# The maxima of the first two query blocks, computed inside the projection stage instead of at the head of the attention stage

## The reference, cut to what matters

```python
q = (x @ Wq).reshape(b, n, 4, 4, 32); k = (x @ Wk).reshape(b, n, 4, 32); v = ...
scores = einsum('bqgsd,bkgd->bgsqk', q, k) / sqrt(32)
scores = where(key > query, -inf, scores)
attn = softmax(scores, axis=-1)
ctx = einsum('bgsqk,bkgd->bqgsd', attn, v).reshape(b, n, 512)
x = layernorm(x + ctx @ Wo + bo)
mu_n = mu / max(sqrt(sum(mu * mu, axis=0)), 1e-12)      # one length per slot, 16 x 128 slots
```

## Time and profile before

| | us |
|---|---|
| median of 3 runs | 2527.34 (2526.09 to 2530.71) |
| the profiled execution, its own time | 2529.19 |
| its span in the profile | 2527.5 |
| projections, until the barrier | 0 to 167.8 |
| attention, until the last product of context and its way out | 167.8 to about 1170 |

### The profile page before, as it was taken

How to read it: one execution, slowest core, us unless ns; L and a number is a source line. 1 busy time by engine, 2 the same in 40 slices (tenths; PEclk the granted TensorE clock), 3 DMA queues, 4 the chain that set the end, 5 groups by cost and what they waited for, 6 DMA issues and landing times. The chain is left out here.

```text
span 2527.5 us, 39129 instructions
## 1 busy us (share of the span) xinstructions
PE 2426.7 (96%) x13026; PEld 1731.5 (69%) x13026; DVE 1738.8 (69%) x3805; ACT 1427.4 (56%) x2764; POOL 1758.0 (70%) x1723
## 2 busy tenths in 40 slices
PE   8989999999999999996978999999999997999998
PEld 6865555555555555543767888877888886788886
DVE  3338888888888888833876656566656564867776
ACT  3214566666666666663865655566656563454553
POOL 4403979898989999897957676675575765555553
PEclk9988999999999999998989999999999998999999
DMA  7861121212222121103964445476444457664553
GB/s 250 271 199 34 40 62 40 62 46 61 57 53 54 50 52 47 49 9 123 361 199 146 160 133 167 138 222 186 142 151 151 144 161 248 190 224 132 148 152 101
DMA packets 232666, 329.58 MB, mean 130 GB/s; under 512 B 56560, under 2 KB 102672, under 8 KB 228240
## 3 DMA queue, kind: packets, MB, share of 16 engines
q1 hardware_dynamic: 195856, 283.47, 36.8%
q0 software_dynamic: 35968, 43.06, 5.8%
q10 hardware_dynamic: 640, 0.55, 0.1%
HBM read 180.63 MB, written 112.22 MB: 116 GB/s over the span
## 5 line engine op out<-in xcount | busy, mean ns | idle before, releaser
L1033 ACT ACTIVATE p_probs<-p_ps_s 128x512 f32<-128x512 f32 (+3 forms) x1280 | 588.9, 540 | 325.8 <-PE p_ps_s L955 320.9
L1624 POOL DMA_DIRECT2D p_eT<-p_ex x1024 | 538.5, 535 | 274.7 <-DVE p_ex L1890 222.1
L884 POOL TENSOR_TENSOR p_added<-p_added,p_probs 128x2048 f32<-128x2048 f32 x136 | 623.9, 4587 | 10.8
L1064 DVE TENSOR_REDUCE p_parts<-p_ps_m 128x1 f32<-128x512 f32 x768 | 468.8, 678 | 45.4 <-PE p_ps_m L942 44.2
L955 PE MATMUL p_ps_s<-q,k_e 98*128 98x512 f32 (+3 forms) x1280 | 472.9, 389 | 3.5 <-ACT p_probs L1033 3.3
L942 PE MATMUL p_ps_m<-k_m,q 96*128 96x512 f32 (+3 forms) x1280 | 455.0, 386 | 7.7 <-PEq L2165 3.9
L955 PEld LDWEIGHTS p_ps_s<-q,k_e 98*128 98x128 f32 x1280 | 241.9, 191 | 180.3 <-issue 82.9
L942 PEld LDWEIGHTS p_ps_m<-k_m,q 96*128 96x128 f32 x1280 | 245.8, 194 | 79.2 <-DVE p_parts L1064 23.6
L973 PE MATMUL p_ps_c<-p_probs,v_e 128*32 128x512 f32 (+3 forms) x2560 | 276.7, 539 | 1.8 <-POOL p_probs L864 1.8
L2024 POOL TENSOR_TENSOR p_acc<-p_acc,logit 128x512 f32<-128x512 f32 x112 | 164.2, 1466 | 151.1 <-ACT logit L2077 147.7
L1068 DVE CUSTOM_DVE_ANT_0 p_masked<-p_ps_m,p_mask 128x384 f32<-128x384 f32 (+3 forms) x512 | 220.5, 485 | 53.7 <-PE p_ps_m L942 47.1
(11 more groups left out here) (193 smaller groups left out, 4772.5 us busy)
## 6 DMA issues: line engine op xcount, KB each, us to landing
logits_t<-logit SPq DMA_DIRECT2D x32, 1024.0 KB, 5.0
p_eT<-p_ex POOLq DMA_DIRECT2D x1024, 32.0 KB, 2.0
logit<-logits_t SPq DMA_DIRECT2D x128, 256.0 KB, 3.4
q<-q_t SPq DMA_DIRECT2D x96, 256.0 KB, 4.7
c_first<-L_ffn_W_dram SPq DMA_DIRECT2D x64, 256.0 KB, 5.6
p_x<-L_attn_x_dram SPq DMA_DIRECT2D x32, 256.0 KB, 5.2
q_t<-p_f_hi SPq DMA_DIRECT2D x32, 256.0 KB, 5.5
q_t<-p_f_lo SPq DMA_DIRECT2D x32, 256.0 KB, 5.6
```

The lines of the kernel that those rows point to most:

```text
L884: pool.tensor_tensor(a[:, :, :], first[:, :, :], probs[s % RING][:, :, :], ALU.add).then_inc(s_add, 1)
L1033: act.activation(probs[s % RING][:, h, q0:BLK], ps_s[:, u % ST_BANKS, q0:BLK], ACT.Exp).then_inc(s_exp, 1)
L1064: dve.tensor_reduce(to, bank, AX.X, ALU.max).then_inc(s_taken, 1)
L1624: pool.dma_start(eT[r][p * QD:(p + 1) * QD, i, :, :], ex[i * QD:(i + 1) * QD, 2 * r:2 * r + 2, bass.ts(p, P)]).then_inc(s_eT[r], 16)
```

## The change

- The constant AHEAD = 2 names the query blocks whose maxima move. Their 48 units (U0 = 48) leave the planner's list and stand in the projections instead, spread over 36 places: behind each chunk c of the groups m = 2 to 5 of block 6 and m = 0 to 4 of block 7. They use the banks `ps_t`, free after the transposes of the last block. The first four wait for VectorE's `xT_lo`, and each later one for the fourth unit before it.
- VectorE does the 48 reductions and both blocks' `maximum_rows` in the projections, each group's reductions ahead of that group's `f_lo`. Mask and scratch lie in an input tile that is no longer used, and GpSimd writes the mask there after its sums.
- The rows of block 0 go out on SP's queue inside the last block's stores (4 DMAs), those of block 1 on ScalarE's at the end of the stage (4 DMAs).
- The attention list starts with unit 48 and with the scores of step 0. `slot_lengths` is now in the plan, after unit 95, in a `ps_m` bank; VectorE copies it out, and GpSimd takes it to the power -0.5 after it has normalised block 1. The load of Wo and the store of the lengths stand behind the context store of block 2 on SP's queue. ScalarE no longer takes a root.
- The semaphore of the first loads is split by block, so a unit or a score waits for its own block only; the wait for all stores is put in front of TensorE's first context product.

```diff
--- before.py
+++ after.py
@@ -94,6 +94,11 @@
         m_in = [al.sbuf(f"p1_mu{j}", [P, DC, EQ * S]) for j in range(2)]
+        mask, masked = x_in[0][:, 0, :], [x_in[0][:, 1 + r, :] for r in range(3)]
+        parts = [al.sbuf(f"p1_parts{n}", [P, 16, QB]) for n in range(AHEAD)]
+        pairs = al.sbuf("p1_pairs", [P, 16, 2])
+        split = al.sbuf("p1_split", [P, 32], F32R)
+        s_row, rows = early
         ps_t = al.psum("p1_ps_t", DC)
...
@@ -117,8 +125,24 @@
+        places = [(NBLK - 2, m, c) for m in range(2, VT + 1) for c in range(DC)] + [(NBLK - 1, m, c) for m in range(VT) for c in range(DC)]
+
+        def units_behind(blk, m, c):
+
+            if (blk, m, c) not in places:
+                return []
+            at, count = places.index((blk, m, c)), M_END[AHEAD - 1]
+            return list(range(at * count // len(places), (at + 1) * count // len(places)))
+
         block = ctx.enter_context(nc.Block())
         x_b = x.rearrange("b n c -> (b n) c")
+
+        def send_rows(eng, n):
+
+            eng.wait_ge(s_max, n + 1)
+            for a in range(4):
+                to = first[0][QROWS:MROWS, n, :, :].rearrange("o h (t a j) -> o h t a j", t=4, a=4)[:, :, :, a, :]
+                eng.dma_start(to.bitcast(F32), rows[n][a * 32:(a + 1) * 32, :]).then_inc(s_row[n], 16)
...
@@ -132,6 +156,8 @@
                 for m in range(NF):
+                    if blk == NBLK - 1 and m == 2:
+                        send_rows(sp, 0)
                     for half, src, ready, done in ((0, f_hi, s_fhi, s_ohi), (1, f_lo, s_flo, s_olo)):
...
@@ -194,6 +220,11 @@
                     load_mu(k + 2)
+            pool.wait_ge(s_xt, (NBLK - 3) * DC)
+            pool.memset(mask, 0.0).then_inc(s_mask0, 1)
+            pool.wait_ge(s_mask0, 1)
+            pool.affine_select(out=mask[:, BLK - P:], in_=mask[:, BLK - P:], compare_op=ALU.is_ge, fill=MASKED,
+                               base=0, pattern=[[-1, P]], channel_multiplier=1).then_inc(s_mask, 1)
             pool.wait_ge(s_mst, 16 * 8)
...
@@ -238,7 +269,24 @@
                                             xT_hi[j][:, c, :], xT_lo[j][:, c, :], c == 0, c == DC - 1)
+                        for u in units_behind(blk, m, c) if c < DC - 1 else []:
+                            unit(u)
                     last.then_inc(s_f, 1)
+                    for u in units_behind(blk, m, DC - 1):
+                        unit(u)
+
+            def unit(u):
+
+                n, c, t, h = MAXU[u]
+                w = unit_width(u)
+                if t == 0 and h == 0 and c == n:
+                    pe.wait_ge(s_first[c], 160)
+                if u < DC:
+                    pe.wait_ge(s_xlo, (NBLK - 1) * DC + u + 1)
+                else:
+                    pe.wait_ge(s_taken, u - DC + 1)
+                pe.matmul(ps_t[:, u % DC, 0:w], first[0][0:QROWS, n, h, bass.ts(t, P)], first[1][:, c * BLK:c * BLK + w],
+                          start=True, stop=True).then_inc(s_unit, 1)
...
@@ -291,6 +339,8 @@
                 values(blk)
+            for n in range(1, AHEAD):
+                send_rows(act, n)
...
@@ -308,6 +358,9 @@
                 for m in ms:
+                    for c in range(DC):
+                        for u in units_behind(blk, m, c):
+                            maximum(u)
                     dve.wait_ge(s_fhi, blk * NF + (m + 1))
...
@@ -320,6 +373,35 @@
                 dve.tensor_copy(v_out[blk % 2][:, :, :], ps_f[:, (FB * blk + V) % 4, :]).then_inc(s_v, 1)
+
+            def maximum(u):
+                n, c, t, h = MAXU[u]
+                w = unit_width(u)
+                to, bank = parts[n][:, h * 4 + t, c:c + 1], ps_t[:, u % DC, 0:w]
+                dve.wait_ge(s_unit, u + 1)
+                if c < n:
+                    dve.tensor_reduce(to, bank, AX.X, ALU.max).then_inc(s_taken, 1)
+                else:
+                    if u == 0:
+                        dve.wait_ge(s_mask, 1)
+                    if u >= 3:
+                        dve.wait_ge(s_taken, u - 2)
+                    dve.tensor_tensor_reduce(masked[u % 3][:, 0:w], bank, mask[:, BLK - w:], 1.0, -3.0e38, ALU.add, ALU.max,
+                                             to).then_inc(s_taken, 1)
+                if u + 1 == M_END[n]:
+                    maximum_rows(n)
+
+            def maximum_rows(n):
...
+                dve.transpose(rows[n][:, :], split[:, :].bitcast(F32)).then_inc(s_max, 1)
...
@@ -331,6 +413,9 @@
                 features_lo(blk, range(2, NF))
+                for c in range(DC):
+                    for u in units_behind(blk, VT, c):
+                        maximum(u)
             values(NBLK - 1)
...
@@ -355,6 +440,9 @@
 MOVING = 4
+AHEAD = 2
+U0 = M_END[AHEAD - 1]
+FIRST_MASKED = min(u for u in range(U0, NU) if MAXU[u][1] == BLOCKS[MAXU[u][0]][1])
...
@@ -433,6 +521,7 @@
         self.work, self.moves = [], []
+        self.rows.update((n, 0.0) for n in range(AHEAD))
         self.groups, self.stall = 0, {"m": 0, "s": 0, "c": 0, "r": 0}
...
@@ -505,6 +594,14 @@
             self.moves.append((self.maxed[u], "maxima keys", (it + 1, c)))
+
+    def lengths(self):
+        self.matmul(self.bank_free(), P)
+        self.pe += 1000
+        self.work.append(("lengths", 0, None))
+        self.dve = max(self.dve, self.pe + self.LAND + self.HOP) + 150
+        self.freed.append(self.dve)
+        self.work.append(("flip lengths", 0, None))
...
@@ -675,6 +772,8 @@
             u += 1
+            if u == M_END[AHEAD]:
+                k.lengths()
         elif add_up:
...
@@ -828,13 +932,16 @@
                 sp.wait_ge(s_ov[j], 16 * NBLK // 2)
-            sp.wait_ge(s_nsum, 1)
-            sp.dma_start(w_raw[:, :, :], Wo.rearrange("(g p) c -> p g c", p=P)).then_inc(s_wo, 16)
             for _, what, a in transfers():
...
                     store(a)
+                    if a == AHEAD:
+                        sp.wait_ge(s_nsum, 1)
+                        sp.dma_start(w_raw[:, :, :], Wo.rearrange("(g p) c -> p g c", p=P)).then_inc(s_wo, 16)
+                        sp.wait_ge(s_ninv, 1)
+                        sp.dma_start(d["inv"], n_inv[:, :]).then_inc(s_nout, 16)
                     if a == NBK - QB:
...
@@ -914,6 +1022,10 @@
                     normalise(a)
+                    if a == AHEAD - 1:
+                        pool.wait_ge(s_pow, 1)
+                        pool.wait_ge(s_flip, flips_to("lengths", 0))
+                        pool.tensor_tensor(n_inv[:, :], n_max[:, :], power[:, :], ALU.pow).then_inc(s_ninv, 1)
                     if a in WEIGHT_BLOCKS:
...
@@ -939,6 +1051,8 @@
                         pe.wait_ge(s_km[c], 48 * it)
+                if t == 0 and h == 0 and it == 0 and c == 0:
+                    pe.wait_ge(s_first[qb], 160)
                 pe.matmul(ps_m[:, bank("maximum", u), 0:w], q[0:QROWS, qb, h, bass.ts(t, P)], k_m[:, c * BLK:c * BLK + w],
...
@@ -948,7 +1062,9 @@
                     pe.wait_ge(s_row[qb], 64 * it + 64)
-                    if it > 0:
+                    if it == 0:
+                        pe.wait_ge(s_first[qb], 160)
+                    else:
                         pe.wait_ge(s_ke[qb], 48 * it)
...
@@ -994,23 +1110,27 @@
             def slot_lengths():
+                at = bank("lengths", 0)
                 pe.wait_ge(s_ones, 1)
                 pe.wait_ge(s_nin, 16)
                 for e in range(E):
-                    mm = pe.matmul(ps_c[:, 0, e:e + 1], mu_sq[:, bass.ts(e, S)], ones[:, 0:1], start=True, stop=True)
+                    mm = pe.matmul(ps_m[:, at, e:e + 1], mu_sq[:, bass.ts(e, S)], ones[:, 0:1], start=True, stop=True)
                 mm.then_inc(s_nsum, 1)
-            pe.wait_ge(s_first, 16 * 10 * QB)
             for what, a, h in order():
                 if what == "maximum":
-                    if a == 12:
-                        slot_lengths()
                     unit(a)
+                elif what == "lengths":
+                    slot_lengths()
                 elif what == "scores":
...
                     if a == 0:
-                        pe.wait_ge(s_nlen, 1)
+                        for m in range(GROUPS + 1):
+                            pe.wait_ge(s_ohi[m], 16 * NBLK)
+                            pe.wait_ge(s_olo[m], 16 * NBLK)
+                        for j in range(2):
+                            pe.wait_ge(s_ov[j], 16 * NBLK // 2)
                     context(a)
...
@@ -1038,10 +1158,6 @@
-            act.wait_ge(s_nsum, 1)
-            act.activation(n_len[:, :], ps_c[:, 0, 0:E], ACT.Sqrt).then_inc(s_nlen, 1)
-            act.wait_ge(s_ninv, 2)
-            act.dma_start(d["inv"], n_inv[:, :]).then_inc(s_nout, 16)
             for what, a, h in order():
...
@@ -1107,15 +1225,12 @@
-            dve.wait_ge(s_mask, 1)
             for what, a, h in order():
                 if what == "maximum":
                     maximum(a)
-                    if a == 23:
-                        dve.wait_ge(s_nlen, 1)
```

(6 more changed lines are left out.)

71 lines of the change are left out of this document (45 added, 26 removed).

## The result

The changed kernel takes 2515.5 us (median of 8 runs, 2510.9 to 2523.5) against 2529.2 us before (8 runs, 2526.1 to 2531.3): ratio 0.9949, 95% interval [0.9935, 0.9962], or 13.7 us less. I had forecast 2508, a gain of 19.9 by its sum, from a kernel before whose median then stood at 2527.3 (3 runs); so 1.9 of the 7.5 us between 2508 and 2515.5 is the kernel before; the gain itself fell short by 6.2 (the sum came to 2507.4). On a second chip the same pair gave 0.9945 [0.9932, 0.9957]. The profiled execution of the changed kernel took 2523.5 us, the longest of its eight.

What follows compares the result with a forecast made beforehand. TensorE, busy 96% of the span, was taken as the bound. 2529.2 less 29.6 at the attention head plus 9.7 in the projections gave 2509.3, 2507.4 on the medians' scale, stated as 2508 us; range 2498 to 2521.

Steps and rivals of the forecast that it cites:

- the 17 us that I gave it: Attention stage: no exp for about 17 us from some 32 us into the stage.
- The projections: Stage before attention: the 48 moved units make it 9.7 us longer, bounds 8 and 14.
- the tie: Projections: VectorE 3.9 us against TensorE 4.0 per full-width group of chunks; 1.1 us added for it.
- My chain through SP: Projections' end: SP's queue ends the stage; 6.0 us of units plus 2.6 for block 0's four row DMAs, 8.6.
- ScalarE's four are beside this: Projections' end: four DMAs on ScalarE's queue lie beside SP's chain and add nothing to it.
- Stretch 1: Head of the attention stage, to the rows of block 2: 48 units, 43 scores, 7 context products; 30.7 us, bounds 27 and 34.
- Stretch 2: Attention stage, run of 28 units after the lengths with one score, set by VectorE: 18.4 us, bounds 17 and 21.
- the one for the lengths: Lengths ahead of the 28-unit run: 3.5 us on TensorE at full clock, filled banks covering 1.8, 1.5 added.
- Stretch 3: Attention stage, from the 28-unit run to the sending of block 3's rows: 31.4 us, bounds 27 and 36.
- The lead is kept: Attention stage after block 3's rows: both lists run on with TensorE full, lead unchanged, 3 us either way.
- the mark: Issue of block 3's rows, where both lists read alike: 80.5 us into the attention stage against 110.1, 29.6 less.
- a tenth of its time free later: Attention stage: GpSimd's mask and power of the lengths cost nothing, as it has a tenth of its time free.
- The middle rival, half the gain: Projections 14 more and stretch 3 at 36 us: 2516 us; with stretch 1 at 34, 2520; chance 0.14.

Runs made afterwards that it cites:

- x4: Changed kernel with block 0's row DMAs in a gap of ScalarE's, half of block 1's on SP, and the lengths' power at block 9's normalisation: 0.9946, 2517.9 us.
- x3: Changed kernel with AHEAD = 1, so only block 0's 16 units stand in the projections: 0.9968, 2523.0 us.
- x0: The changed kernel unaltered, run again with a second profile: 0.9945, 2518.8 us on a chip where the kernel before takes 2532.7.
- x11: Changed kernel with one matmul in place of the sixteen of the slot lengths, fifteen sums left out (results wrong): 0.9928.
- x2: Changed kernel with the slot lengths moved behind block 7's rows, and GpSimd's power and the two DMAs hanging on them at block 6: 0.9929.
- x7: Changed kernel with GpSimd's adds of blocks 0 to 4, from each block's third tile on, cut to a quarter of their columns (sums wrong): 0.9928, 2513.5 us.
- x10: Changed kernel with GpSimd's power of the lengths moved right behind VectorE's copy of the lengths out of their bank: 0.9923.
- x8: The kernel before, unaltered, with a second profile; rows of block 3 at 281.2 us instead of 277.9.
- x9: Changed kernel with x4's row DMAs, block 0's late sums issued as soon as ready, and the power right behind VectorE's copy of the lengths: 0.9901, 2506.6 us.

## Why the prediction was right in sign and 7.5 us off

**The mechanism** was as forecast: exps start with the stage (177.85), they pause, the projections pay TensorE's time for the units at full clock. The pause is longer than the 17 us that I gave it: but for one exp at 210.04 there is none from 204.6 to 233.95 us.

**The projections**: 9.7 forecast, 8.8 measured. The 8.3 us of the units on TensorE is the term that counts: its last transposes start at 172.51 instead of 163.23, 9.3 later, with the 1.0 of the tie. My chain through SP came to nearly the same number and is not the cause: SP's stores and TensorE's values met within half a microsecond (x4), and SP decided only in x3, with fewer units and its rows done late. "ScalarE's four are beside this" was wrong by 0.8 to 1.1 us.

**Stretch 1**: 30.7 forecast, 30.4 measured, with VectorE at 27.54 of 30.40 (0.91, I took 0.90).

**Stretch 2**: 18.4 forecast, 22.3 measured (and more in x0). This is the step that failed. TensorE in the changed kernel:

```profile
204.27 5.31 PE L1117 MATMUL p_ps_m<-p_ones,p_w_o 128*128 128x1 f32 x32
209.44 0.56 PE L1071 MATMUL p_ps_s<-q,k_e 98*128 98x256 f32 x1
209.80 1.05 PE L1056 MATMUL p_ps_m<-k_m,q 96*128 96x512 f32 x2
210.79 1.94 PE L1089 MATMUL p_ps_c<-p_probs,v_e 128*32 128x512 f32 x8
```

VectorE at the same place:

```profile
209.62 0.17 DVE L1233 TENSOR_SCALAR p_slot_length<-p_ps_m 128x16 f32<-128x16 f32 x1 [2.69 <-PE p_ps_m L1117]
210.47 1.29 DVE L1180 TENSOR_REDUCE p_parts<-p_ps_m 128x1 f32<-128x512 f32 x2 [0.67 <-PE p_ps_m L1056]
213.49 1.29 DVE L1180 TENSOR_REDUCE p_parts<-p_ps_m 128x1 f32<-128x512 f32 x2 [1.73 <-PE p_ps_m L1056]
216.49 13.24 DVE L1180 TENSOR_REDUCE p_parts<-p_ps_m 128x1 f32<-128x512 f32 x22 [1.71 <-PE p_ps_m L1056]
```

VectorE waits 6.8 us (2.69 + 0.67 + 1.73 + 1.71) where I gave it 1.5. Its 28 maxima end at 230.93, so counted on VectorE, as the sum was, stretch 2 took 23.9 us and stretch 3 31.0. The term that failed is the one for the lengths, 3.5 us of which 1.5 were to reach VectorE: I priced them at full clock, and what stands behind them too, though the earlier trace rows showed the clock at half inside them. They took 5.3, and the half clock went on over the matmuls that feed VectorE. One thing more was missing: I counted seven products before this stretch and seven behind it, and the four in it (steps 7 to 10, 5.4 us of TensorE's here) stood in no term. x11 shows that this omission cost nothing. It has the same four products, and without fifteen of the matmuls and the half clock behind them VectorE runs its 28 maxima without a wait:

```profile
207.70 16.82 DVE L1180 TENSOR_REDUCE p_parts<-p_ps_m 128x1 f32<-128x512 f32 x28
```

That is the 16.9 of my sum (in x2 it is 16.79). In x0 VectorE waits 8.8 us, and its 28 maxima end at 233.21. In x7, where the clock held to the end of the lengths (3.67 us) and was at half for 3.4 us behind them, it waits 3.7.

**Stretch 3**: 31.4 forecast, 32.6 measured from TensorE's last lone unit, within its bounds.

**"The lead is kept"**: 16.0 at the mark, 10.2 at the end of the attention stage, outside my 3 either way; in x0 13.0 and 10.1, just inside them. I had excluded GpSimd by its share ("a tenth of its time free later"). It gained less from the change than TensorE: its 11th to 17th add start 8 to 9 us earlier than before, where TensorE is 15 ahead; and it was given 2.94 us of power that I had priced at nothing. x7 and x10 show that without the one or the other the loss is gone. The 3 us or so that the clock cost at 322 us are in one of the changed kernel's two profiles.

**In sum**, of the 19.9 forecast: 0.9 better in the projections and 0.3 in stretch 1, 3.9 worse in stretch 2 and 1.2 in stretch 3 make the 16 of the mark (counted on VectorE, 5.5 worse in stretch 2 and 0.4 better in stretch 3); 5.8 are lost behind it. That leaves the 10.2 of this pair of profiles; x0 and x8 lie 14.2 apart at the last context product, and the medians 13.7. The middle rival, half the gain, gave nearly the measured time (2516) by other terms: the projections and stretch 3 were as forecast, and what it doesn't name was lost. That it met the time is luck.

## What to carry to other kernels

When work is taken out ahead of the engine that sets the pace, ask of each other engine how much earlier it gets. The one that gets less is the next wait, even where its busy share leaves a tenth free. Price a row at the clock that the row shows, and ask what clock it leaves behind: a handful of narrow matmuls, and some short stops, cost more than their own time. And work moved "where an engine is idle" is free only if nothing in that engine's queue behind it is waited for (x9).
